# A Mamba block with a quantised product: PSUM's banks dealt out anew, and the order of every engine's work with them

## The reference, cut to what matters

```python
xz = norm(x) @ in_proj_w.T;  xi, z = split(xz)            # 1024 channels each
xc = silu(conv4(xi) + conv_b)                             # over positions, 4 taps
xp = xc @ x_proj_w.T                                      # 1 + 16 + 16 columns
delta = softplus(xp[:, 0:1] * dt_w + dt_b);  B, C = xp[:, 1:17], xp[:, 17:33]
# in chunks of 128 positions, for each of the 16 states s, a_s = exp(A_log[s]):
log_A_cum = cumsum(max(-a_s * delta, log(EPS)))           # over the chunk's positions
wcum      = cumsum(delta * B[s] * xc / max(exp(log_A_cum shifted), EPS))
h_s       = exp(log_A_cum) * wcum / A_bar + h_in * exp(log_A_cum)
y        += C[s] * h_s
out = x + (y + D * xc) * silu(z) @ out_proj_w.T;  out += int8_product(norm(out), rhs)
```

## Time and profile before

| | us |
|---|---|
| median of 3 runs (5843.09 to 5845.2) | 5843.38 |
| span of the profiled execution | 5836.6 |
| TensorE busy | 5616.2 |
| VectorE busy | 5351.4 |
| ScalarE busy | 3734.7 |
| GpSimd busy | 2457.2 |

### The profile page before, as it was taken

The page is one execution under the profiler, slowest core; times in us unless marked ns, Lnnn a source line. Parts: engine busy times, 40 slices in busy tenths (PEclk is TensorE's granted clock), DMA queues, the critical chain, the costliest instruction groups (busy, mean ns, idle before and its releaser), DMA issues. The chain is left out here.

```text
span 5836.6 us, 78230 instructions
## 1 busy us (share of the span) xinstructions
PE 5616.2 (96%) x16088; PEld 2643.7 (45%) x16152; DVE 5351.4 (92%) x7057; ACT 3734.7 (64%) x4618; POOL 2457.2 (42%) x2139
## 2 busy tenths in 40 slices
PE   5999999999999999999999999999999999999998
PEld 2444444444444444444444444444444444444443
DVE  4999999999999999999999999999999999999997
ACT  3666666666666666666666666666666666666664
POOL 2444444444444444444444444444444444444443
PEclk9999999999999999999999999999999999999999
DMA  1122121121121211212212112112122121121220
GB/s 68 12 18 20 15 18 16 15 20 16 15 19 14 18 17 15 20 16 15 20 14 17 17 17 18 16 15 20 14 17 19 14 18 16 15 20 16 15 18 12
DMA packets 157893, 104.23 MB, mean 18 GB/s; under 512 B 121008, under 2 KB 121008, under 8 KB 157488
## 3 DMA queue, kind: packets, MB, share of 16 engines
q1 hardware_dynamic: 157488, 100.71, 19.0%
HBM read 42.63 MB, written 16.78 MB: 10 GB/s over the span
## 5 line engine op out<-in xcount | busy, mean ns | idle before, releaser
L487 POOL TENSOR_SCALAR room<-total,limit 128x1024 f32<-128x1024 f32 x1024 | 1183.1, 1155 | 3245.6 <-PE cum L1038 475.3
L739 ACT ACTIVATE decay<-cum,neg_a 128x1024 f32<-128x1024 f32 x1024 | 1137.3, 1111 | 1543.0 <-PE cum L1038 1539.3
L1048 PE MATMUL state<-sources,tri_upto 128*128 128x512 f32 x4096 | 1971.5, 604 | 123.9 <-DVE term L1380 123.5
L1038 PE MATMUL cum<-step,tri_before 128*128 128x512 f32 x4096 | 1938.8, 596 | 3.5 <-DVE sources L1367 3.5
L1380 DVE SCALAR_TENSOR_TENSOR term<-state,crow,decay 128x1024 f32<-128x1024 f32 x1024 | 1312.6, 1282 | 312.9 <-PE state L1048 196.0
L1390 DVE TENSOR_TENSOR acc<-acc,term 128x1024 f32<-128x1024 f32 x1024 | 1359.2, 1327 | 0.2
L1367 DVE SCALAR_TENSOR_TENSOR sources<-cum,brow,dx 128x1024 f32<-128x1024 f32 x1024 | 1305.5, 1275 | 10.0 <-ACT cum L755 10.0
L1038 PEld LDWEIGHTS cum<-step,tri_before 128*128 128x128 f32 x4096 | 781.1, 192 | 966.3 <-issue 943.7
L755 ACT ACTIVATE cum<-room,pos_a 128x1024 f32<-128x1024 f32 x1024 | 1143.6, 1117 | 110.6 <-POOL room L487 101.8
L1048 PEld LDWEIGHTS state<-sources,tri_upto 128*128 128x128 f32 x4096 | 743.3, 190 | 994.3 <-issue 867.3
L476 POOL TENSOR_SCALAR step<-delta,limit 128x1024 f32<-128x1024 f32 x1024 | 1144.7, 1118 | 8.3 <-PE cum L1038 7.0
(11 more groups left out here) (127 smaller groups left out, 3630.5 us busy)
## 6 DMA issues: line engine op xcount, KB each, us to landing
hfirst<-hrows SPq DMA_DIRECT2D x496, 64.0 KB, 3.9
xt<-in_x SPq DMA_DIRECT2D x64, 256.0 KB, 2.6
hrows<-term SPq DMA_DIRECT2D x1024, 4.0 KB, 1.6
xres<-in_x SPq DMA_DIRECT2D x64, 256.0 KB, 2.7
out_x<-xres SPq DMA_DIRECT2D x64, 256.0 KB, 2.1
gate_last<-gate SPq DMA_DIRECT2D x512, 0.5 KB, 2.0
win<-in_w_in SPq DMA_DIRECT2D x2, 2048.0 KB, 10.8
hrows<-hrows SPq DMA_DIRECT2D x64, 64.0 KB, 2.3
```

The lines of the kernel that those rows point to most:

```text
L487: nc.gpsimd.tensor_scalar(room[:, :], total[:, :], limit[:, s:s + 1], 0.0, ALU.min, ALU.max).then_inc(limited, 1)
L739: nc.scalar.activation(decay[s % 4][:, :], cum[s % 2][:, :], ACT.Exp, scale=neg_a[:, s:s + 1]).then_inc(decay_ready, 1)
L1038: last = nc.tensor.matmul(cum[s % 2][:, cols], tri_before[:, :], step[s % 2][:, cols], start=True, stop=True)
L1048: last = nc.tensor.matmul(state[:, cols], tri_upto[:, :], source[s % 2][:, cols], start=True, stop=True)
```

## The change

`cum` gets one pair of banks, `state` two pairs by `s % 2`, and `growth` is written into the pair in which the same slot's state will stand; `room` gets a second buffer in SBUF, paid for by laying `ones`, `csel` and `qT` over other arrays. The waits follow: `states(s)` waits for `source(s)` alone, `cumulate(s)` for `decay(s-1)`, `growths(s)` for `term(s-2)`. All the orders are changed:

- TensorE: `states(s)`, front and end pieces, `cumulate(s+2)`.
- ScalarE: `decays(s+1)`, `growths(s+1)`, then the rest; `decay_once` goes from slot 15 to 14.
- VectorE: `term(s-1)`, `add(s-1)`, the extras, `source(s+1)`.
- GpSimd: `limit_step(s+3)`, then `limit_sum(s+2)`; in slots 2 and 9 `turn` waits for `added(s-2)`.

```diff
-        cum = [ps(f"cum{i}", [P, DI]) for i in range(2)]
-        state = ps("state", [P, DI])
+        cum = ps("cum", [P, DI])
+        state = [ps(f"state{i}", [P, DI]) for i in range(2)]
+        growth = state
+        carry_state = state[1]
...
# GpSimd, body
                     turn(t, s, more, more2)
-                    if s + 2 < NS and s + 2 in ROOM_POOL:
-                        limit_sum(t, s + 2)
...
                     if s + 3 < NS:
                         limit_step(t, s + 3)
...
+                    if s + 2 < NS:
+                        limit_sum(t, s + 2)
...
# ScalarE
             def growths(t, s):
-                act.wait_ge(decay_ready, slot_at(t, s))
...
+                user, old = before(t, s, 2)
+                if user is not None:
+                    act.wait_ge(term_ready, slot_at(user, old))
...
-                    ahead, slot = (t, s + 2) if s + 2 < NS else (nxt, s + 2 - NS)
+                    ahead, slot = (t, s + 1) if s + 1 < NS else (nxt, 0)
...
# TensorE
             def cumulate(t, s):
                 pe.wait_ge(step_ready, slot_at(t, s))
-                user, old = before(t, s, 2)
+                user, old = before(t, s, 1)
                 if user is not None:
-                    pe.wait_ge(source_ready, slot_at(user, old))
+                    pe.wait_ge(decay_ready, slot_at(user, old))
...
             def states(t, s):
                 pe.wait_ge(source_ready, slot_at(t, s))
-                user, old = before(t, s, 1)
-                if user is not None:
-                    pe.wait_ge(term_ready, slot_at(user, old))
...
                 for s in range(NS):
-                    if s + 2 < NS:
-                        cumulate(t, s + 2)
+                    states(t, s)
...
-                    states(t, s)
+                    if s + 2 < NS:
+                        cumulate(t, s + 2)
...
# VectorE, body
                         term_of(prev, NS - 1)
-                    if s + 1 < NS:
-                        source_of(t, s + 1)
...
                     if s > 0:
                         add(t, s - 1)
...
                             end_scale(prev)
+                    if s + 1 < NS:
+                        source_of(t, s + 1)
```

More of the change, by code:

```diff
@@ L177, in mamba_block @@
         step = [sb(f"step{i}", [P, DI]) for i in range(2)]
-        room = sb("room", [P, DI])
+        room = [sb(f"room{i}", [P, DI]) for i in range(2)]
         sources = sb("sources", [P, 2, DI])
@@ L795, in start @@
                 decay_once(t)
[L796 to L800, removed]
+                decays(t, 0)
+                growths(t, 0)
             def body(t, more, more2):
@@ L813, in body @@
                             front_square(nxt)
[L814 removed]
+                        if s == 14:
                             decay_once(nxt)
[L816 to L818 removed]
+                    if more or s + 1 < NS:
                         decays(ahead, slot)
@@ L822, in body @@
                         finish(prev)
+                    if more or s + 1 < NS:
+                        growths(ahead, slot)
                     if more:
@@ L840, in body @@
                             end_guess(prev)
-                    if more or s + 2 < NS:
-                        growths(ahead, slot)
                     if prev2 is not None and s == 0:
@@ L900, in _ @@
                 pe.wait_ge(consts_dve, 7 + j)
-                last = nc.tensor.matmul(ebank[:, j * P:(j + 1) * P], ones[:, :], rdiags[j], start=True, stop=True)
+                last = nc.tensor.matmul(ebank[:, j * P:(j + 1) * P], ones, rdiags[j], start=True, stop=True)
             last.then_inc(consts_pe, 1)
@@ L1042, in states @@
                 pe.wait_ge(source_ready, slot_at(t, s))
-                user, old = before(t, s, 1)
-                if user is not None:
-                    pe.wait_ge(term_ready, slot_at(user, old))
                 for h in range(2):
                     cols = slice(h * HALF, (h + 1) * HALF)
-                    last = nc.tensor.matmul(state[:, cols], tri_upto[:, :], source[s % 2][:, cols], start=True, stop=True)
+                    last = nc.tensor.matmul(state[s % 2][:, cols], tri_upto[:, :], source[s % 2][:, cols], start=True, stop=True)
                 last.then_inc(state_ready, 1)
@@ L1058, in finish @@
                         for cols in halves:
-                            last = nc.tensor.matmul(state[:, cols], tri_upto[:, :], carried[:, cols], start=True, stop=True)
+                            last = nc.tensor.matmul(carry_state[:, cols], tri_upto[:, :], carried[:, cols], start=True, stop=True)
                         last.then_inc(carry_sums, 1)
@@ L1063, in finish @@
                         for cols in halves:
-                            last = nc.tensor.matmul(state[:, cols], csel[:, :], hend[t.parity][:, cols], start=True, stop=True)
+                            last = nc.tensor.matmul(carry_state[:, cols], csel, hend[t.parity][:, cols], start=True, stop=True)
                         last.then_inc(carry_products, 1)
@@ L1366, in source_of @@
                 dve.wait_ge(growth_ready, slot_at(t, s))
-                nc.vector.scalar_tensor_tensor(out=source[s % 2], in0=cum[s % 2][:, :], scalar=brow[t.parity][:, s:s + 1],
+                nc.vector.scalar_tensor_tensor(out=source[s % 2], in0=growth[s % 2][:, :], scalar=brow[t.parity][:, s:s + 1],
                                                in1=dx[t.parity][:, :], op0=ALU.mult, op1=ALU.mult).then_inc(source_ready, 1)
```

82 lines of the change are left out of this document (35 added, 47 removed).

## The result

The changed kernel takes 6521.35 us (median of 3 runs, 6506.64 to 6526.87) against 5843.38: a ratio of 1.115, 95% interval 1.113 to 1.117, slower. Forecast were 6440, in a range of 5980 to 6570. The profiled execution's span is 6504.6 us, its mean granted clock 0.975 (before 5836.6 and 0.992).

A forecast was written before the change was run, and what follows sets the result against it. TensorE and VectorE were taken as nearly full, their orders deciding how far one runs ahead. Slots with the lock 98.55 plus loop 0.45 gave 99.0 us a tile against 89.4, over 62 tiles 595 us more: 6440 us, range 5980 to 6570.

The forecast's parts named there:

- the walk: Sum of the lengths of a tile's sixteen slots: 91.4 us without the GpSimd-VectorE lock, 98.55 with it.
- TensorE's slow groups: Matmul groups lengthened after a TensorE stall of 2 to 3 us: taken as 0, at most 1 us a tile.
- Part 1: `states(s)` no longer waits for `term(s-1)`: if nothing replaced that wait, a gain of 220 us.
- Parts 2 to 4: Handshake of at least 3.9 us between states, dependent pair, waits of single slots: 91.4 us a tile.
- dependent pair: VectorE's term and add directly behind each other start 1.39 us apart: 0.19 more a slot, 3.0 a tile.
- part 4: Waits in single slots, such as 3, 7, 9, 10 and 14, summed over sixteen slots: 91.4 us a tile.
- rival C: VectorE keeps its lead across slots 3, 7 and 14; slot 4 under 4.9 us; 5760 us; chance 0.08.
- Part 5: GpSimd's clips and VectorE's two-operand SBUF work exclude each other: tile of 98.55 us in place of 91.4.
- The sign that I named for `delta`: VectorE's `delta`, with adds, taps and `carry_first`, would show a mean well over its usual length (1.25 us).
- Rival B: Lock hardly bites: VectorE's next operation passes the waiting one, or GpSimd finds its gap; 6010 to 6130 us; chance 0.27.
- Part 6: Loop's return: VectorE's remaining 2.0 us falls in slot 0 of every second tile, 0.45 a tile (bounds 0 and 1.3).
- TensorE idle in front of `state`: TensorE waits for VectorE's source near 13 us a tile, mostly before states 5, 7 and 15.

The follow-up runs named there:

- Short clips: GpSimd's clips `step` and `room` cut to 64 of 1024 columns, flag's branch kept closed: on the changed kernel 6193.07 us, on the kernel before 5741.69 us.
- No branch: Branch `other_carries` with its block taken out of all five engines: on the changed kernel 6362.82 us, on the kernel before 5851.62 us.

## Why the prediction held, and where it was off

The forecast's mechanism is for the most part the one measured: a shorter handshake, and the lock between GpSimd and VectorE on top of it. The sum was made of 98.55 for the walk and 0.45 for the loop; measured, a tile without a return takes 97.53, and the mean over both kinds is 2.52 above that. That 99.0 came so near to 100.05 is in part luck: the walk was too long, and two terms, TensorE's slow groups and the loop, were too small.

- **Part 1.** Right: TensorE's wait for a term is gone as a releaser of `state`. The ceiling of 220 us was never in reach.
- **Parts 2 to 4, the walk without the lock: 91.4.** Short clips' other tile is 91.49, against 86.97 for the same treatment of the old order: handshake, dependent pair and single slots cost 4.5 a tile. Slot by slot, too, the short clips' tile is the walk of part 4 to within 0.25, but for slot 0 (6.0 put, 5.55) and slot 14 (5.3, 5.90). The pairs are 1.38 apart (3115.09, 3116.47); 1.39 was put. In the kernel after, slot 7's chain came as put:

```profile
3140.61 1.28 ACT L840 ACT_TABLE_LOAD   x1
3141.91 1.11 ACT L734 ACTIVATE decay<-cum,neg_a 128x1024 f32<-128x1024 f32 x1
```

decay(9) starts 6.9 after `state(7)` (3134.99; 7.0 was put) and `state(9)` 10.5 after it (3145.46; 10.6). So VectorE keeps no lead, and slot 4 takes 6.89, and 5.92 with short clips: rival C, which needed under 4.9 there, is dead with and without the lock.
- **Part 5, the lock.** 97.53 - 91.49 = 6.0 a tile where the walk had 98.55 - 91.4 = 7.15. By slot (put, measured over the same sixteen slots as the windows above): 4: 6.4, 6.89; 6: 7.4, 7.03; 11: 7.3, 6.98; 12: 6.45, 5.53; 13: 6.1, 6.91; 14: 6.2, 6.28; 3: 6.75, 5.95; 9: 6.65, 6.16; 0: 6.3, 5.72; all sixteen 98.55, 96.64 (the mean of a tile without a return is 97.53). Slots 0, 3, 9 and 12 lost less than I had put. The sign that I named for `delta` failed: it kept its length (1246), and the loss came in the add of the next slot, 13 (2.12 in one row). Rival B said that the waiting operation would be passed over: adds with a mean of 1453, `room` with 1651 and the run of short clips refute it. What I missed is that the old order paid for the clips as well, 99 us, by the lock or by ScalarE's wait for `room`.
- **Part 6, the loop: the first term that was mis-sized.** I put 0.9 a pass, 0.45 a tile (bounds 0 to 1.3). The returning tile is 5.45 longer than the other, half of that a tile, 2.7. I had followed only VectorE's 3.15 and found its remainder, 2.0, correctly. I had not followed TensorE and ScalarE over `finish(prev)`: before, both came to it with `cumulate(2)`, decay and growth queued ahead; now it stands directly behind `state(0)` on TensorE, and ScalarE's growth(1) has a wait, new with the change, for VectorE's way past it. No branch shows the size: the difference between the two kinds of tile falls from 5.45 to 1.44, and the time by 158 us, while leaving the branch out gives the old order nothing. (97.53 - 98.55) + (2.52 - 0.45) = 1.05 a tile, or 65 us of the 81 by which 6521 is over 6440; the walk was 1.0 too long, the loop 2.1 too short.
- **Part 6, TensorE's slow groups: the second term that was mis-sized.** I took them as 0, at most 1 a tile, since behind the stalls of slots 4 and 14 VectorE would set the pace. The same slot 5 in two tiles of the kernel after, timeline of TensorE and windows of TensorE (columns as in the earlier trace rows):

```profile
3122.14 1.98 PE L1025 MATMUL state<-sources,tri_upto 128*128 128x512 f32 x4 [2.34 <-DVE sources L1344]
...
3218.78 2.70 PE L1025 MATMUL state<-sources,tri_upto 128*128 128x512 f32 x4 [2.34 <-DVE sources L1344]
```

```profile
3122.14:3127.96 5.82, 5.82 (x16) 1.00 0.31 13
3218.78:3226.16 7.38, 7.38 (x16) 0.77 0.25 12
```

The stall is the same, 2.34, but in the second tile a part of slot 5 ran at the lower level of the clock, 1.2 GHz, and the slot is 1.56 longer (slot 6 wins back 0.47 of it). Of 56 tiles in the loop, 26 have such a slot 5 and 21 such a slot 15 (6.8 to 6.95 in place of 5.47): about 1.0 a tile. This is why tiles without a return take from 96.3 to 98.8, with a mean of 97.53; those with neither take 96.3 or 96.6, so the walk proper was some 2 too long, not 1.0. With short clips none of the 56 tiles has such a slot; there TensorE stands 1.35 and 1.53 on the mean in front of states 5 and 15, where it stands 2.32 and 2.24 in the kernel after. So about 1 of the 6.0 a tile under part 5 is this: the lock makes these stalls longer, and the slow groups follow.
- **TensorE idle in front of `state`:** near 13 a tile were put, with source as the releaser, most of it in front of states 5, 7 and 15. The releaser (480.9 us in 389 waits) and the places (5.7 of the 7.8) are right, the size is not: 7.8 a tile. A part of the rest shows as busy time: over the sixteen slots of the windows TensorE is busy for 88.69 (before, in the same way, 86.84), and its `state` pieces have a mean of 626 in place of 604 ns.

The waits of the kernel after, beside these:

```profile
PE state L1025 <- DVE sources L1344: 480.9, 389, 3.0
ACT state L744 <- DVE term L1357: 414.6, 319, 3.0
...
ACT state L744 <- DVEq L275: 127.5, 57, 4.0
PE fbank L911 <- PEq L275: 104.8, 29, 4.1
```

The last row is what was missing in part 6: 3.6 us in each of the 29 passes.

So the 678 us divide: 4.5 a tile (some 280) for the shorter handshake and the dependent pair, 5.3 (some 330) for the clips beyond what the old order paid for them, in tiles without a return, and 0.8 (some 50) more through the return. Short clips' difference of 229 is less than 330 because their returning tiles differ from the others by 7.9 in the new order (5.45 with whole clips) and by 1.9 in the old one (3.6): what the clips cost and what the return costs overlap, so the shares are not exact.

The Trainium skill, page "SBUF — State Buffer", section "SBUF: two separate sides", states the exclusive lock between VectorE and GpSimd: the one that starts first keeps the shared ports for its whole instruction, and the other waits. The rows of slots 4, 6 and 14 agree with it (2.08 for 1.11, 0.96 for a product of eight columns, 3.07 for 1.23).

## What to carry to other kernels

When buffers are dealt out anew, what decided here is how far each engine may still run ahead: the handshake of 3.9 us fitted inside every slot, but each extra in front of it then counted, with the dependent pair 4.5 us a tile. Where GpSimd works beside VectorE on operands in SBUF, place it under VectorE's operations that read PSUM: here that place alone was worth 289 us. Follow every engine over a loop's return and over each branch near it, and ask what it has queued ahead; a closed branch whose removal won nothing in one order cost 158 us in another.

## What the runs showed of the hardware

- A closed branch (flag loaded, compared, jumped over) right behind the loop's return kept TensorE standing 3.64 us, and the groups after it took 2.81 and 2.61 in place of 1.88, at a granted clock of 0.69 over the stretch: for a part of it the lower of the two levels, 1.2 GHz. With four tiles a pass in the old order it stood 2.1 to 2.6 us at such a branch where no loop returned.
- The same stall of 2.34 us in front of `state(5)` of the kernel after was followed once by a group of 1.98 and once by one of 2.70 (granted clock of the slot 1.00 and 0.77). In no branch a stall of 2.59 was followed by groups of 1.98 and 1.88 (1.00), and one of 2.34 by a group of 3.58 (0.58). The idle time alone doesn't tell which it will be.
- GpSimd's clip of 64 columns (`step`) took 317 ns on the mean in the old order (`room` 508 in the new one, where it also waits for VectorE), where 1024 columns take 1.11 us: a sixteenth of the columns takes over a quarter of the time.
- A tiny operation pays for the lock like a large one: the product of eight columns took 0.96 us behind a waiting clip.
